# Attention and mixture-of-experts kernel: products of the jobs in four 32-column tiles, the whole first batch scored in fp32 from 32 rows, and a new order of the jobs

## The reference

```python
x = x + attn(layernorm(x))            # 8 heads of 16
x = x + ffn(layernorm(x))
# attn: Q, K, V, U = silu of x @ W; s = (Q K^T + bias[i - j]) / 4, causal, keys that are all zero masked
#       out = (silu(s) @ V) * U       silu stands where a softmax would
# ffn:  y = sum over 8 experts of gate[e] * (x @ w_in[e].T @ w_out[e].T), gate of the two largest logits
```

## Time and profile before

| | |
|---|---|
| median of 3 runs | 306.09 us (304.94 to 306.87) |
| profiled execution, its own time | 303.84 us |
| span of the profiled execution | 302.1 us |
| TensorE (PE) busy | 273.6 us (91%), 1860 matmul records |
| VectorE (DVE) busy | 230.4 us (76%) |
| ScalarE (ACT) busy | 230.7 us (76%) |
| GpSimd (POOL) busy | 150.0 us (50%) |
| moved by DMA | 36.32 MB |

### The profile page before, as it was taken

How to read it: one execution, slowest core, us unless ns; L and a number is a source line. 1 busy time by engine, 2 the same in 40 slices (tenths; PEclk the granted TensorE clock), 3 DMA queues, 4 the chain that set the end, 5 groups by cost and what they waited for, 6 DMA issues and landing times.

```text
span 302.1 us, 5983 instructions
## 1 busy us (share of the span) xinstructions
PE 273.6 (91%) x1860; PEld 131.8 (44%) x1860; DVE 230.4 (76%) x757; ACT 230.7 (76%) x468; POOL 150.0 (50%) x243
## 2 busy tenths in 40 slices
PE   1899968989989999999999999999989999999781
PEld 0545543345455534534344434443334555544430
DVE  5238711872688985899999986878999999795877
ACT  2766945999997889789998889997658769768510
POOL 6355300521080258518661289547557297398281
PEclk9999997999999999999999999999999999999997
DMA  6967699779346904970477037715670010010101
GB/s 176 225 185 166 174 211 232 211 205 215 97 123 215 190 5 158 212 149 12 126 188 202 0 83 215 158 29 165 145 188 0 2 38 0 3 35 2 35 1 35
DMA packets 30670, 36.32 MB, mean 120 GB/s; under 512 B 3240, under 2 KB 17064, under 8 KB 30640
## 3 DMA queue, kind: packets, MB, share of 16 engines
q1 hardware_dynamic: 27232, 33.53, 44.3%
q10 hardware_dynamic: 3408, 2.43, 3.7%
HBM read 23.87 MB, written 12.08 MB: 119 GB/s over the span
## 4 chain that ended last, share of the span: by engine, by line
PE 62%; DVE 18%; ACT 12%; issue 5%; POOL 2%; DMA 1%; DVEq 0%; ACTq 0%; POOLq 0%
PE o_acc L631 16%; PE jobp L700 14%; PE score L614 13%; DVE score L884 8%; PE jobp L664 7%; ACT wts L755 4%; ACT wts L753 3%; ACT xn L768 3%; PE jobp L655 2%; DVE ymix L980 2%; PE jobp L693 2%; PE jobp L713 2%; PE jobp L672 2%; PE jobp L687 2%; DVE lg L1020 1%
## 5 line engine op out<-in xcount | busy, mean ns | idle before, releaser
L884 DVE TENSOR_TENSOR score<-score,bias_near 128x256 f32<-128x256 f32 (+3 forms) x288 | 113.5, 466 | 15.2 <-PE score L614 14.9
L753 ACT ACTIVATE wts<-score 128x512 f32<-128x512 f32 (+2 forms) x200 | 98.5, 532 | 25.5 <-DVE score L884 22.2
L560 POOL TENSOR_TENSOR ymix<-ymix 128x512 f32<-128x512 f32 (+2 forms) x90 | 74.1, 823 | 51.5 <-DVE ymix L980 46.8
L755 ACT ACTIVATE wts<-score,far 128x512 f32<-128x512 f32 x120 | 74.1, 699 | 10.9 <-PE o_acc L631 4.2
L631 PE MATMUL o_acc<-wts,v_pad 128*32 128x512 f32 (+3 forms) x864 | 79.4, 464 | 1.1 <-ACT wts L753 0.9
L700 PE MATMUL jobp<-mm_e,xn2T 128*128 128x512 f32 x120 | 62.9, 628 | 1.4 <-DVE ymix L980 1.3
L614 PE MATMUL score<-q_stack,k_stack 64*128 64x256 f32 (+3 forms) x400 | 60.4, 367 | 3.2 <-issue 2.7
L614 PEld LDWEIGHTS score<-q_stack,k_stack 64*128 64x128 f32 x400 | 35.3, 185 | 41.0 <-issue 33.4
L980 DVE TENSOR_TENSOR ymix<-jobp,gates 128x512 f32<-128x512 f32 x60 | 40.3, 684 | 13.8 <-PE jobp L700 13.1
L700 PEld LDWEIGHTS jobp<-mm_e,xn2T 128*128 128x128 f32 x120 | 19.2, 189 | 30.5 <-issue 21.6
L768 ACT ACTIVATE xn<-xs,shift,rstd 128x128 f32<-128x128 f32 x64 | 26.4, 491 | 7.8 <-POOL shift L506 7.8
(11 more groups left out here) (83 smaller groups left out, 258.4 us busy)
## 6 DMA issues: line engine op xcount, KB each, us to landing
k_stack<-rows_dram SPq DMA_DIRECT2D x32, 256.0 KB, 5.2
q_stack<-rows_dram SPq DMA_DIRECT2D x28, 256.0 KB, 6.3
rows_dram<-k_hi SPq DMA_DIRECT2D x16, 256.0 KB
xs<-in_L_attn_x SPq DMA_DIRECT2D x8, 256.0 KB, 8.7
rows_dram<-k_lo SPq DMA_DIRECT2D x8, 256.0 KB
rows_dram<-q_hi SPq DMA_DIRECT2D x7, 256.0 KB
rows_dram<-q_lo SPq DMA_DIRECT2D x7, 256.0 KB
out<-xs SPq DMA_DIRECT2D x7, 256.0 KB, 4.5
```

The lines of the kernel that those rows point to most:

```text
L560: then_wait(pool.tensor_tensor(y[:, 0:n], y[:, 0:n], y[:, n:2 * n], ALU.add))
L753: act.activation(weights, score[bank][:, 0:n], ACT.Silu, scale=HD ** -0.5).then_inc(weighed[bank], 1)
L755: act.activation(weights, score[bank][:, 0:n], ACT.Silu, bias=far[:, h:h + 1], scale=HD ** -0.5)\
L884: ins = dve.tensor_tensor(score[bank][:, c + near:c + n], score[bank][:, c + near:c + n], bias, ALU.add)
```

## The change

1. **Quarters.** The products of `Q`, `K`, `U`, `V`, `MASK`, `LOG`, `FF` and `M` are written as four matmuls of 32 stationary columns each, into four 32-partition parts of the bank. The transposes (`T1`, `T2`, `SEL`, `WT`) stay as they are.
2. **Batch 0 in fp32.** Unit 1 is scored like unit 0, from `kpad` and Q in fp32 with 32 rows for a head. `kpad` now has both halves of the keys and lies in the memory of x of batches 2 and 3; batch 0's Q lies in `xn2T`. Batch 0's three splits, their row writes and stack loads are gone, and x of batch 2 is loaded only when group 19 is scored.
3. **Order.** The bias table is read back ahead of expert 1. `BEFORE`, `BESIDE` and `AFTER` are new throughout: `Q` of the second half and `REL` leave the prologue, the experts' `WT` and `M` stand earlier, `U` and `V` of batch 1 later.

```diff
-            _names = [("o", _u), ("v", _b, _kb // HT)] + ([("q", _b, _half), ("k", _b, _kb // HT)] if _u > 0 else [])
+        if _b == 0:
+            FIRST_KEYS.setdefault((_quad, _kb // HT), _group)
+        for _name in [("o", _u), ("v", _b, _kb // HT), ("q", _b, _half), ("k", _b, _kb // HT)]:
...
-SPLITS = [(0, 0, 1), (0, 1, 0), (0, 1, 1)]
-SPLITS += [(b, half, side) for b in range(1, B) for half in range(2) for side in (1, 0)]
+SPLITS = [(b, half, side) for b in range(1, B) for half in range(2) for side in (1, 0)]
...
 BEFORE = [
-    [("stats1", 0, 0), ("RB",), ("stats1", 0, 1), ("norm1", 0, 0), ("T1", 0, 0), ("WT", 0), ("norm1", 0, 1),
-     ("K", 0, 0), ("V", 0, 0), ("T1", 0, 1), ("U", 0, 0), ("Q", 0, 0), ("Q", 0, 1), ("split", 0, 0), ("K", 0, 1),
-     ("MASK", 0, 0), ("REL",)],
+    [("stats1", 0, 0), ("RB",), ("norm1", 0, 0), ("T1", 0, 0), ("norm1", 0, 1), ("stats1", 0, 1), ("WT", 0),
+     ("Q", 0, 0), ("T1", 0, 1), ("K", 0, 0), ("V", 0, 0), ("K", 0, 1), ("U", 0, 0), ("MASK", 0, 0)],
 ]
 BESIDE = [
-    [("split", 0, 1), ("V", 0, 1), ("stats1", 1, 0)],
+    [("stats1", 1, 0), ("M", 0), ("V", 0, 1)],
+    [("Q", 0, 1), ("U", 0, 1), ("stats1", 1, 1)],
+    [("WT", 1), ("norm1", 1, 0), ("REL",), ("WT", 2)],
+    [("M", 1), ("MASK", 0, 1)],
+    [("WT", 3), ("T1", 1, 0)],
+    [("K", 1, 0), ("Q", 1, 0), ("split", 1, 0)],
...
+    [("MASK", 1, 1), ("norm2", 1), ("FF", 0, 2, 0), ("SEL", 2), ("FF", 0, 2, 1), ("stats2", 2), ("best", 1, 0),
+     ("FF", 0, 3, 0), ("T2", 1), ("LOG", 1), ("norm1", 2, 1)],
...
+        first_q = [xn2T[:, half * HALF:(half + 1) * HALF] for half in range(2)]
+        kpad = xs[:, B - QUADS:B].rearrange("p b t d -> p b (t d)")
...
-            load_expert(1)
             sp.wait_ge(ext_out, 16)
...
-            write_rows(0, 0, 1)
+            load_expert(1)
             load_x(1, 0)
-            load_stack(0, 0, 1)
-            write_rows(0, 1, 0)
-            write_rows(0, 1, 1)
-            load_stack(0, 1, 0)
-            load_stack(0, 1, 1)
             load_x(1, 1)
...
+                if b == 1:
+
+                    wait_all_scored(sp, last_use(("k", 0, 1)) + 1)
+                    load_x(2, 0)
+                    load_x(2, 1)
...
+            def quarters(out, lhsT, rhs, start=True, stop=True):
+
+                for c in range(4):
+                    rows = slice(32 * c, 32 * c + 32)
+                    ins = pe.matmul(out[rows], lhsT[:, rows], rhs, start=start, stop=stop)
+                return ins
...
-                    ins = pe.matmul(bank[:], xn2T[:, t * P:(t + 1) * P],
+                    ins = quarters(bank[:], xn2T[:, t * P:(t + 1) * P],
                                     mm_e[:, part * E // 2:(part + 1) * E // 2, :].rearrange("p e d -> p (e d)"),
                                     start=True, stop=True)
...
+                    cols = slice(args[1] * HALF, (args[1] + 1) * HALF)
                     for quad in range(QUADS):
-                        dve.tensor_scalar(kpad[:, quad], qk32[1][:, 0:HALF], parity[:, quad:quad + 1], None, ALU.mult)\
+                        dve.tensor_scalar(kpad[:, quad, cols], qk32[1][:, cols], parity[:, quad:quad + 1], None, ALU.mult)\
                             .then_inc(kpad_ready, 1)
```

More of the change, by code:

```diff
@@ L206 @@
[L206 to L214, removed]
[13 rows of a table added]
+    [("M", 4), ("LOG", 0), ("best", 0, 0), ("best", 0, 1)],
+    [("M", 5), ("MASK", 1, 0)],
@@ new lines @@
+    [("WT", 6), ("WT", 7)],
+    [("M", 6)],
+    [("tanh", 0)],
+    [],
+    [],
[8 rows of a table added]
+    [("tanh", 1), ("V", 2, 0), ("best", 1, 1), ("gates", 1), ("T1", 2, 1)],
+    [("FF", 0, 3, 1), ("FF", 0, 4, 0), ("FF", 0, 4, 1), ("norm2", 2)],
+    [("FF", 0, 5, 0)],
+    [("FF", 0, 5, 1), ("T2", 2)],
+    [("LOG", 2), ("K", 2, 1), ("best", 2, 0)],
+    [("stats1", 3, 0), ("FF", 0, 6, 0), ("stats1", 3, 1), ("MASK", 2, 0)],
+    [("FF", 0, 6, 1)],
+    [("MASK", 2, 1)],
+    [("Q", 2, 1), ("split", 2, 1)],
@@ L218 @@
-    [],
-    [("best", 7, 0), ("LOG", 7)],
[2 rows of a table added]
+    [("LOG", 7)],
+    [("best", 7, 0), ("best", 7, 1)],
     [],
@@ L531, in split_lo @@
                 cols = slice(half * HALF, (half + 1) * HALF)
-                for side in ((1, 0), (0, 1))[(b, half) == (0, 1)]:
-                    if (b, half, side) not in SPLIT:
-                        continue
+                for side in (1, 0):
                     pool.wait_ge(hi_ready, SPLIT[b, half, side] + 1)
@@ L662, in job_pe @@
                     rows = xn1T[:, half * HALF:(half + 1) * HALF]
-                    ins = pe.matmul(bank[:], w[:], rows[:, ::-1] if kind == "Q" else rows, start=True, stop=True)
+                    ins = quarters(bank[:], w[:], rows[:, ::-1] if kind == "Q" else rows, start=True, stop=True)
                 elif kind == "V":
@@ L671, in job_pe @@
                         t = HT * half + k
-                        ins = pe.matmul(bank[:, k * D:(k + 1) * D], xn1T[:, t * P:(t + 1) * P], wv_s[:],
+                        ins = quarters(bank[:, k * D:(k + 1) * D], xn1T[:, t * P:(t + 1) * P], wv_s[:],
                                         start=True, stop=True)
@@ L680, in job_pe @@
                         t = HT * half + k
-                        ins = pe.matmul(bank[:, k * H:(k + 1) * H], kabs[:, t * P:(t + 1) * P], headsum[:],
+                        ins = quarters(bank[:, k * H:(k + 1) * H], kabs[:, t * P:(t + 1) * P], headsum[:],
                                         start=True, stop=True)
@@ L692, in job_pe @@
                     for k, t in enumerate(tiles):
-                        ins = pe.matmul(bank[:, k * E:(k + 1) * E], xn2T[:, t * P:(t + 1) * P], wg_s[:],
+                        ins = quarters(bank[:, k * E:(k + 1) * E], xn2T[:, t * P:(t + 1) * P], wg_s[:],
                                         start=True, stop=True)
@@ L712, in job_pe @@
                     for c in range(HC):
-                        ins = pe.matmul(bank[:, 0:D], expert_in(e)[1][:, c, :], woutT[:, e % 2, c, :],
+                        ins = quarters(bank[:, 0:D], expert_in(e)[1][:, c, :], woutT[:, e % 2, c, :],
                                         start=(c == 0), stop=(c == HC - 1))
@@ L786, in job_act @@
                             act.wait_ge(lo_ready, SPLIT[b - 1, half, side] + 1)
-                        if (b - 1, half, side) == (0, 0, 0):
-                            wait_all_scored(act, last_use(("o", 0)) + 1)
+                        if side and b == 1:
+                            act.wait_ge(kpad_ready, QUADS * (half + 1))
                         if side:
@@ L792, in job_act @@
                     cols = slice(half * HALF, (half + 1) * HALF)
-                    drained_by(act.activation(qk32[side][:, cols], bank_of(job)[:], ACT.Silu), job)
+                    dst = first_q[half] if (b, side) == (0, 0) else qk32[side][:, cols]
+                    drained_by(act.activation(dst, bank_of(job)[:], ACT.Silu), job)
                     if side:
```

122 lines of the change are left out of this document (55 added, 67 removed), and 42 rows, old and new, of tables (AFTER, BESIDE).

## The result

| | before | after |
|---|---|---|
| median | 305.83 us (4 runs, 304.94 to 306.87) | 292.31 us (4 runs, 291.95 to 294.28) |
| profiled execution, its own time | 303.84 us | 292.33 us |
| span | 302.1 us | 290.6 us |
| TensorE busy | 273.6 us | 266.8 us, 3124 matmul records |
| moved by DMA | 36.32 MB | 31.24 MB |

The ratio is 0.957, with a 95% interval of 0.9517 to 0.9623: faster by 13.5 us of the median, where 8.4 were forecast. The two profiled executions are 11.5 us apart.

The account below looks back on a forecast made before the run. TensorE was taken as the bound from group 20 to 79, shared with ScalarE in groups 6 to 20, nothing full before. Stretch terms of -1.2, -4.8, +3.0, 0, -1.6 and -3.5 sum to -8.1 us: 297.7 us forecast, range 290 to 304.

Parts of the forecast that it names:

- The likeliest case: Whole kernel: a time of 293 to 301.5 us, given a chance of 0.60.
- the fourth rival: Start closes up fully and TensorE's saving is all real: -17.6 us, 288.5 at its end, 291 in its middle; chance 0.13.
- The floor of 21 us: Groups 0 to 5: ScalarE's work in steps 0 to 5 adds to 21 us, TensorE's to 20.
- I allow for filling the pipeline as in the first steps, 23.7: Groups 0 to 5: 23.7 us instead of the floor of 21, so -4.8 us (-1 to -7) from 28.49.
- two engines at 41 to 42 with longer scores between them: 46.7: Groups 6 to 19: TensorE 42.0 and ScalarE about 41 us of work, stretch 46.7, so +3.0 us (-1 to +8).
- Groups 40 to 59: TensorE's work -2.5 us, ScalarE and VectorE rising to about 52 and 55: time -1.6 us (0 to -3).
- its sign of being wrong: TensorE waiting more for ScalarE or VectorE from group 20 on, or groups 6 to 19 taking over 50 us.
- Quarters: TensorE's work: -7.4 us from changes of form, +0.9 for wide products, -5.1 for LOG, 0 for MASK.
- x of batch 2 late: Load waits for group 19, stats two to three steps (6 us) later: 0, or 3 us if it lands after 9 us.
- The first: Narrow quarters are bound by issue at 62 ns a matmul: +38.7 us, so 336.7 us; chance 0.05.
- The second rival: Unit 1's heads come two by two, a second round per group: 11.3 us instead of 3, so 309 us; chance 0.08.
- The third: After group 20 ScalarE or VectorE binds, so -5.1 us shrinks to -1: 302 us; chance 0.14.

Follow-up runs that it names:

- e6_fp32_early_x: Kernel before, old order, whole products, unit 1 in fp32, batch 2's x loaded after group 12 and ahead of batch 1's second stacks: 305.03 us, ratio 1.0017.
- e11_log_whole: Changed kernel with the LOG products whole, all others in quarters: 297.9 us, ratio 0.9811.
- e5_expert_first: Changed kernel with expert 1 queued ahead of the bias table again: 292.04 us, ratio 0.9584.
- e7_early_x: Changed kernel with batch 2's x load waiting for group 12 only, still behind the stacks in the queue: 291.96 us, ratio 0.9587.
- e3_fp32: Kernel before, whole products, old order, unit 1 in fp32, bias table ahead of expert 1, batch 2's x and its first jobs later: 320.44 us, ratio 1.0498.

## Why the prediction was right, and by how much it was off

The sign and the range (290 to 304) held. The likeliest case, 293 to 301.5 us, did not: 292.31 lies just below it, between it and the fourth rival. The forecast was 5.4 us too high. Of that, 2.0 are in the step from the profiled execution to the median: I added the 2.25 us by which the median stood above it, and the changed kernel's profiled execution is its median. The runs of one kernel spread by about 2 us here (304.94 to 306.87, 291.95 to 294.28), so that step was chance. The other 3.4 are the sum by stretch, -11.5 instead of -8.1, and there is luck in that: groups 0 to 19 came out 6.8 us better than forecast and groups 20 to 59 2.2 us worse.

- **Prologue**, -1.2 forecast, -0.5 measured. The Q job has left; what took the other 0.7 was not looked into.
- **Groups 0 to 5**, -4.8 forecast, -7.75 measured. The floor of 21 us was right as a number (20.74), but not its engine: it was ScalarE's sum, and ScalarE had 18.24 us to do, while TensorE, put at 20, had 20.55. The step that failed is "I allow for filling the pipeline as in the first steps, 23.7". It was measured as the order before left it, and in that order it is there: `e6_fp32_early_x` has 24.41. The new order takes the gaps and some waits of the scores out. I also put this gain on the missing stall and clock; those are worth 4.1 us (28.49 to 24.41, fp32 scores included), and the order 3.4.
- **Groups 6 to 19**, +3.0 forecast, -0.8 measured. TensorE's sum of 42.0 was right (42.73). The step that failed is "two engines at 41 to 42 with longer scores between them: 46.7": the allowance of 4.7 measured 0.1. ScalarE had 38.61 us to do and not 41, and the new order leaves TensorE hardly any gap (42.73 of 42.84). The price of fp32 scores in this stretch was +4.6; the scores took 12.0 us before, 18.4 in `e6_fp32_early_x` and 17.6 in the changed kernel, waits for banks included, so +6.4 and +5.6.
- **Groups 20 to 39**, 0 forecast, +0.1 measured, with step 26 at 1.94 us instead of up to 1.5.
- **Groups 40 to 59**, -1.6 forecast, +0.5 measured. TensorE's busy time went up by 0.5 instead of down by 2.5. The step that failed is taking that 2.5 of saved work for saved time. The work was priced well: all products but the scores went from 46.3 to 44.1 us. But the same 96 score records went from 14.0 to 17.2 us, by waits for banks that ScalarE and VectorE had not yet emptied. The prediction has no term for those, though it names them as its sign of being wrong.
- **Groups 60 to the end**, -3.5 forecast, -3.0 measured.
- **Quarters** as a term: -7.4 + 0.9 - 5.1 - 0 for MASK, -11.6 us of TensorE's work, measured -11.0 of busy time in the new order. The agreement is luck: the other products lost 14.5 us and the scores took 4.2 back. V products alone lost 7.0 us (73.1 to 66.2), 0.88 us instead of 0.99 with a quartered product behind them; that gain I had not counted. LOG: 5.1 forecast, 5.8 of busy time and 5.6 of time measured, but with seven changes into the 128-column form in it that I had counted elsewhere (37 of them in `e11_log_whole`, 30 in the change). In the order before, the quarters gave 8.7 of busy time, because there the scores took 5.8 back.
- **TensorE as a whole**, -6.4 forecast, -6.8 measured as busy time, which is the same luck: the other products lost 15.4 us (11.6 forecast), the scores gained 9.7 (5.2 forecast).
- **Bias ahead of expert 1, x of batch 2 late, REL in step 2**: the first two at 0 each, as forecast (`e5_expert_first`, `e7_early_x`); the third no run tests alone. The 0 for the late x, which I gave with "the queue holds nothing else behind this wait", left out what stands ahead of it in the queue: in the order before, the late wait, the place behind the stacks and the places of batch 2's jobs together cost 15 us (`e3_fp32` against `e6_fp32_early_x`), where I had said 3 for a load that lands after 9 us.
- **Rivals.** The first fell: V jobs of 32 matmuls at 0.87 us, 27 ns each, and LOG at 9 ns each, so the pace of 62 ns that the Trainium skill gives ("TensorE: Matmul & The Clock Gate", the section on the 56 ns gap) is not that of this kernel. Its advice against tiling a dimension that is already small ("TensorEngine Tiling (Array Packing)", section Instruction Overhead) does not bear on LOG: the tiled side is the 128 stationary columns and only the streamed one is small, and LOG is the job with the largest gain. The second rival is partly there: some scores of unit 1 do take longer than one round (four heads in 1.72 us at 43.38), but fp32 scores cost the stretch of groups 6 to 19 4.3 us in `e6_fp32_early_x`, not the rival's 11.3, and with the new order that stretch is shorter than before. Its 309 us also adds the 11.3 to a sum that keeps the 3 it was to replace; by its own words it is 306. The third is half there: -5.1 forecast from group 20 on, -1 by the rival, -2.4 measured, and the waits of the scores are what it described. The fourth came closest: groups 0 to 5 and 6 to 19 as it said or better, the rest not.

Not tried: the new order with unit 1 from stacks. Whether the order wins its 3.4 us only together with fp32 scores, or alone as well, stays open.

## What to carry to other kernels

When a stretch has gaps in every engine, ask whether they belong to the work or to the order: here an allowance taken from the old order (2.7 and 4.7 us) was the largest error, and the floor of the fullest engine was the better forecast. Four tiles of 32 columns made the fp32 LOG, which streams 8 columns, 2.5 times as fast (all of them 7.6 to 3.0 us, the best 0.99 to 0.29). That fits a product that is paid for by its weight load, but it did not carry over to MASK, which also streams 8 columns and is bf16: 0.18 us whole (18.83 to 19.01 in the kernel before) and 0.19 in quarters. Wide products gain only the change of form, their own and that of the V product ahead of them. A high busy share of TensorE does not say that it never waits: compare groups of the same shape, as the scores here, and if some take twice as long as others, look at what their weight loads wait for. Before a load is moved later, look at what is then ahead of it in its queue, and at what its first reader stands in front of in its engine's program: a late load with its late readers cost 15 us in one order, and a late wait nothing in the other.

## What the runs showed of the hardware that was not expected

- A transposition of a 128x128 fp32 block is one record and a job of four takes 0.59 us (56.99 to 57.58 in the changed kernel); as an fp32 product in four tiles it is two passes and takes 0.99.
- 32 fp32 matmuls with 8 columns each go in 0.29 us, 9 ns a matmul (226.93 to 227.22), with their 32 weight loads in 0.38 us, from 226.90.
- The same quarters took 8.7 us off TensorE's busy time in one order of the jobs and 11.0 in the other, with nearly the same number of changes of form (43 fewer against 45). Without the scores it is 14.9 and 14.5; the difference is in how long scores wait for banks, which the busy time holds.
- Around a pause of TensorE of 12 us (102.10 to 114.06 in `e3_fp32`) the granted clock was 0.75 over 100 to 110 us and 0.50 over 110 to 120, with TensorE busy 5.05 us in the latter; after the pause of 2.65 us in the earlier trace rows the clock was 0.57 over 4 us.
